# A state-space loop on one core: where a group's output is added to x, and the order of two kinds of loads

## The chip, the cores and the metric

The kernel runs on one core of a Trainium2 chip. The metric is the device time of one execution in microseconds. The run shown is one profiled execution; beside it stand three unprofiled ones. All times inside the execution count from the start of its span.

## The reference, cut to what matters

A stack of six layers on x of shape (4, 256, 512), all float32: a mixture-of-experts layer, an attention layer, the same experts again, a SwiGLU layer, a Mamba2 layer, the same SwiGLU again. The change is in the Mamba2 layer:

```python
proj = hidden_states @ in_proj_w.T                  # gate, x/B/C, dt
xBC = silu(conv(xBC) + conv_b)                      # depthwise, 4 taps
scores = einsum('bclhn,bcshn->bchls', C, B) * exp(seg)   # per head, lower triangle
y = scores @ (x * dt) + carried state + x * D
yg = y * silu(gate)
rstd = rsqrt(mean(yg**2 over the 1024 channels of a group) + 1e-5)
out = (yg * rstd * norm_w) @ out_proj_w.T
x = x + out
```

There are 128 heads of 64 channels, in 8 groups of 16 heads. The factor rstd belongs to one token and one group, so it can be applied after the output product: each group's 1024 channels give a (tokens x 512) sum, and this sum times rstd is added to x.

## The kernel before, in words

The 1024 tokens are 8 tiles of 128. The Mamba2 layer is a loop over 8 groups g (NG), each of 8 steps v (TPG); a step handles one pair of heads, 128 channels. All 64 steps are written out in program order on each engine, in a function `step(v, g)` that every engine has its own version of. Matrix products are float32 in three passes of high and low parts.

- **TensorE** (`step` in the block of `pe`): two input products (`chunk`) for the next step's channels; in even steps the second half (tiles 4 to 7) of the output products of the two steps before (`out_products`, half 1), and in step 0 also the sums of squares of the group before; then the attention-like products y of this step (`y_products`); two more chunks; transposes; in odd steps the first half (tiles 0 to 3) of the output products. An output product of a tile goes to one of three PSUM banks (OBANK), so product t + 3 waits until tile t has been read out. Products of the steps (0, 1), (2, 3), (4, 5), (6, 7) are summed in SBUF in `oacc`.
- **VectorE** (`step` in the block of `dve`), in this order: convolution taps (`taps`, L1393) of the first two chunks, in even steps with the read-out (`evacuate`) of tiles 4 to 7 between them; `skip` (L1446) and `gate` (L1455) on y; the low parts `y_lo` (L1461), each behind a high part that ScalarE writes (L913); `decay_off` (L1432), `scale_x` (L1411, L1413) for the next step; in odd steps the read-out of tiles 0 to 3; `decay` (L1439) for the next step, which that step's y products wait for. Step 7 has eight chunks of the next group in place of four.
- **The read-out** of the pair (0, 1) of a group is a copy into `oacc` (L1481), and the other pairs add to it (L1484). As the copy overwrites the sum of the group before, `update(g - 1, t)` (L1469), x + oacc * rstd for one tile, stands directly ahead of each of the eight copies: for tiles 0 to 3 at the end of step 1, for tiles 4 to 7 in step 2. The factor rstd comes in step 0 from TensorE (sums of squares), VectorE (L1489) and GpSimd (L607).
- **ScalarE**: weight high parts (L691), convolution starts (L862), the exponents of the decays (`spans`, L899, then Exp, L906), silu, y high parts.
- **GpSimd**: weight low parts (L551, L557), squares of y (L597, L601, L603), rstd (L607).
- **SyncE** issues all loads in one order (`step` in the block of `sp`): in step v the input weight slabs that TensorE uses from step v + 1 on (`mamba_A`, L363, 256 KB each; two in most steps, four in step 6), then the decay rows of the next step (`mamba_rows`, L404, 1.5 MB, broadcast to all partitions), then in even steps two output weight slabs (`mamba_B`, L373). A slab waits until the products that use its slot's last content are done; the rows wait for the y products of the step before this one.

Of the kernel before, what the change touches and what calls it, by code (L numbers as in the profile page):

```python
# [47 lines left out]
def build(nc, x_in, w0_in, b0_in, lb_in, wqkv_in, wo_in, fa_in, fb_in, ma_in, mb_in, dtw_in, chp_in, cst_in, out):  # L48
# [268 lines left out]
    def next_step(v, g):  # L317
        return (v + 1, g) if v < TPG - 1 else (0, g + 1)

    def step_chunks(v, g, last):  # L320
        if v < TPG - 1:
            return g, [4 + 4 * (v + 1) + c for c in range(4)]
        return g + 1, [] if last else list(range(8))

    def step_tiles(v, last):

        if v < TPG - 2:
            return [2 + 2 * (v + 2), 3 + 2 * (v + 2)]
        if last:
            return []  # L330
        return [NA_G + i for i in (range(4) if v == TPG - 2 else (4, 5))]
# [6 lines left out]
    def _(sp):  # L338
# [50 lines left out]
        def mamba_A(i, g):  # L389

            src = ma_in[g * NA_G + i] if isinstance(g, int) else ma_in[bass.ds(g * NA_G + i, 1)].squeeze(0)
            load_A(A0G + i, src, g, NA_G)

        def mamba_B(i, g):
            src = mb_in[g * TPG + i] if isinstance(g, int) else mb_in[bass.ds(g * TPG + i, 1)].squeeze(0)
            load_B(B0G + i, src, g, TPG)

        def mamba_rows(v, g):

            k = g * TPG + v  # L400
            if not (isinstance(k, int) and k < 2):
                sp.wait_ge(m_y, 2 * (k - 1) + FREE)
            h = slice(2 * k, 2 * k + 2) if isinstance(k, int) else bass.ds(2 * k, 2)
            sp.dma_start(eb[:, v % 2, :, :, :], scr[h].partition_broadcast(P)).then_inc(m_rows[v % 2], 16)  # L404

        def step(v, g, last=False):

            for i in step_tiles(v, last):
                mamba_A(i, g)
            mamba_rows(*next_step(v, g))  # L410
            if v % 2 == 0 and not (last and v == TPG - 2):
                mamba_B(v + 2, g)
                mamba_B(v + 3, g)
# [32 lines left out]
        for g in range(NG - 1):  # L446
            for v in range(1, TPG):
                step(v, g)
            step(0, g + 1)
# [660 lines left out]
    def _(dve):  # L1110
# [260 lines left out]
        def param(g, tile, which):  # L1371
            if tile < 2:
                at = CP_BC + tile * PBC + which
                per = 2 * PBC
            else:
                at = (tile - 2) // 2 * PX + which
                per = TPG * PX
            if isinstance(g, int):
                at = at + g * per
                return chp[:, at:at + 1]  # L1380
            return chp[:, bass.ds(g * per + at, 1)]

        def taps(g, c, which=(1, 2, 3)):

            n = conv_index(g, c)
            acc = conv_acc(g, c).rearrange("p (b l) -> p b l", b=2)
            src = ps[:, chunk_bank(g, c), :].rearrange("p (b l) -> p b l", b=2)
            for j in which:
                if j == 1:
                    dve.wait_ge(m_acc, n + 1)  # L1390
                else:
                    dve.wait_ge(m_tap, 3 * n + j - 1)
                nc.vector.scalar_tensor_tensor(out=acc[:, :, j:S], in0=src[:, :, 0:S - j],  # L1393
                                               scalar=param(g, c // 2, 3 - j), in1=acc[:, :, j:S],
                                               op0=ALU.mult, op1=ALU.add).then_inc(m_tap, 1)
# [21 lines left out]
        def decay_off(v, g, p):  # L1417

            k = g * TPG + v
            if k == 0:  # L1420
                dve.wait_ge(m_first[p], 48)
                dve.wait_ge(m_exp, p + 1)
            elif k == 1:
                dve.wait_ge(m_second, 32)
                dve.wait_ge(m_exp, 3)
            else:
                dve.wait_ge(m_rows[v % 2], 16 * (k // 2 + v % 2))
            if v == 0:
                dve.wait_ge(m_cbm, B * (g + 1))
            e = eb[:, v % 2, :, NT + 2 * p:NT + 2 * p + 2, :].rearrange("p h t q -> p h (t q)")  # L1430
            w = cbO[:, 2 * p:2 * p + 2, :].rearrange("p t q -> p (t q)")
            nc.vector.tensor_tensor(e, e, w.unsqueeze(1).to_broadcast([P, 2, 2 * P]), ALU.mult)  # L1432
# [25 lines left out]
        def y_lo(g, v, p):  # L1458
            half = slice(512 * p, 512 * p + 512)
            dve.wait_ge(m_yhi, 2 * (g * TPG + v) + p + 1 + FREE)  # L1460
            nc.vector.scalar_tensor_tensor(out=yTl[:, v % 2, half], in0=gt[:, v % 2, half],  # L1461
                                           scalar=param(g, 2 + 2 * v, 6), in1=yTh[:, v % 2, half].bitcast(F32),
                                           op0=ALU.mult, op1=ALU.subtract).then_inc(m_ylo, 1)

        def update(g, t):
            if t % 4 == 0:
                dve.wait_ge(m_rstd, g + 1 + FREE)
            dve.wait_ge(m_osum, 32 * g + 24 + t + 1 + FREE)
            nc.vector.scalar_tensor_tensor(out=x[:, t, :], in0=oacc[:, t, :], scalar=rstd[:, t:t + 1],  # L1469
                                           in1=x[:, t, :], op0=ALU.mult, op1=ALU.add).then_inc(x_new, 1)  # L1470

        def evacuate(v, g, t):

            j = v // 2
            done = 8 * j + t + 1
            dve.wait_ge(m_out, g * (NT * TPG // 2) + OB + done)
            if j == 0:
                if not (isinstance(g, int) and g == 0):
                    update(g - 1, t)
                    dve.wait_ge(x_new, g * NT + XB[4] + t + 1)  # L1480
                nc.vector.tensor_copy(oacc[:, t, :], ps[:, OBANK[t % 3], :]).then_inc(m_osum, 1)  # L1481
            else:
                dve.wait_ge(m_osum, 32 * g + done - 8 + FREE)
                nc.vector.tensor_tensor(oacc[:, t, :], ps[:, OBANK[t % 3], :], oacc[:, t, :],  # L1484
                                        ALU.add).then_inc(m_osum, 1)

        def mean_square(g, bank):
            dve.wait_ge(m_ss, g + 1 + FREE)
            nc.vector.tensor_scalar(ss[:, :], ps[:, bank, 0:NT], 1.0 / GROUP, EPS, ALU.mult,  # L1489
                                    ALU.add).then_inc(m_var, 1)  # L1490
# [47 lines left out]
        def step(v, g, last=False, first=False):  # L1538
            gn, todo = step_chunks(v, g, last)
            conv = [c for c in todo if c < 4 or (c // 2) % 2 == 0]  # L1540
            drain = v % 2 == 0 and not first
            before = (v - 1, g) if v else (TPG - 1, g - 1)
            taps(gn, conv[0])
            taps(gn, conv[1], (1,))
            if drain:
                evacuate(*before, 4)
            taps(gn, conv[1], (2, 3))
            if drain:
                for t in range(5, NT):
                    evacuate(*before, t)  # L1550
                if v == 0:
                    mean_square(g - 1, 4)
            ending = last and v == TPG - 2
            if ending:
                decay_off(v + 1, g, 0)
                decay_off(v + 1, g, 1)
            skip(g, v, 0)
            gate(g, v, 0)
            skip(g, v, 1)
            gate(g, v, 1)  # L1560
            if ending:
                decay(v + 1, g, 0)
                decay(v + 1, g, 1)
                scale_x(v + 1, g, 0)
                scale_x(v + 1, g, 1)
            if len(conv) > 2:
                taps(gn, conv[2])
            y_lo(g, v, 0)
            if len(conv) > 2:
                taps(gn, conv[3])  # L1570
            y_lo(g, v, 1)
            if len(conv) > 2:
                taps(gn, conv[4])
                taps(gn, conv[5])
                for b in range(B):
                    mask_cb(gn, b)
            vn = next_step(v, g)
            if not ending and not (first and v == 0):
                decay_off(*vn, 0)
                decay_off(*vn, 1)  # L1580
            if not ending:
                scale_x(*vn, 0)
                scale_x(*vn, 1)
            if v % 2 == 1:
                for t in range(4):
                    evacuate(v, g, t)
            if first and v == 0:
                decay_off(*vn, 0)
                decay_off(*vn, 1)
            if not ending:  # L1590
                decay(*vn, 0)
                decay(*vn, 1)
# [693 lines left out]
```

## Time and profile before

| | |
|---|---|
| median of 3 runs | 2223.58 us (2219.56 to 2225.03) |
| the profiled execution, its own time | 2223.88 us |
| its span | 2222.1 us |
| mean granted TensorE clock | 0.989 |
| busy: TensorE, weight loads | 96%, 79% |
| busy: VectorE, ScalarE, GpSimd | 75%, 65%, 46% |

The span is what the profiler sees; the execution's own time is 1.8 us longer. The loop over groups and steps takes most of the span from 570 to 2010 us, 184 to 186 us a group. A busy share is an average over stages with different limits, so the reading goes stage by stage. A line of the windows view gives a stretch, its length, the busy time (and instructions) of TensorE, its weight loads, VectorE, ScalarE and GpSimd, then the granted TensorE clock, the DMA engines' share and GB/s. A line of the timeline gives start, duration, engine, source line, operation, tiles and, in brackets, the idle time before it with what ended it. "ps" are the PSUM banks, "wBh,yTh" an output product, "xTh,wAh" an input product, "eb,xdt" a y product.

### The profile page before, as it was taken

To read this page: it belongs to the slowest core of one execution; us is meant where nothing else is said; L and a number is where in the kernel's file an instruction comes from. 1 tells how busy PE (TensorE), PEld (TensorE's weight loads), DVE (VectorE), ACT (ScalarE), POOL (GpSimd) and SP (SyncE) were. 2 spreads that over 40 slices of the span, in tenths; PEclk is the share of its full clock that TensorE was granted. 3 is DMA by queue.
4 is the path that set the end of the run, shared out by engine and by line. 5 is a ranking of instruction groups with operands and counts; after the bars stand their busy time and mean duration, and the time that the engine had idled before them with its cause. 6 is when DMAs were issued, how large, how long until landed. Compare 5 with 4: busy or idle time off the path is not lost.

```text
span 2222.1 us, 34801 instructions
## 1 busy us (share of the span) xinstructions
PE 2141.8 (96%) x12604; PEld 1750.1 (79%) x12604; DVE 1660.0 (75%) x2661; ACT 1434.2 (65%) x3090; POOL 1031.9 (46%) x755
## 2 busy tenths in 40 slices
PE   7989889999999999999999999999999999998999
PEld 7866678887788878878878887887887888787887
DVE  7777673225888898899889889889888988987121
ACT  4488643335978767668776776767867677683332
POOL 5577445352354345344454434534445443454442
PEclk9999999999999999999999999999999999999999
DMA  3000012331432323233224232323322432231332
GB/s 133 1 1 2 1 44 86 95 93 54 153 131 102 110 95 109 94 120 117 93 86 142 94 117 86 109 99 115 124 86 86 143 106 104 86 110 48 95 95 81
DMA packets 65337, 202.53 MB, mean 91 GB/s; under 512 B 7056, under 2 KB 9104, under 8 KB 56976
## 3 DMA queue, kind: packets, MB, share of 16 engines
q1 hardware_dynamic: 65168, 200.31, 26.6%
q8 instruction: 102, 1.67, 0.3%
q14 instruction: 67, 0.55, 0.1%
HBM read 197.39 MB, written 2.88 MB: 90 GB/s over the span
## 4 chain that ended last, share of the span: by engine, by line
PE 74%; DVE 12%; ACT 8%; issue 4%; DMA 1%; POOL 0%; SPq 0%; DVEq 0%; ACTq 0%; POOLq 0%
PE ps L1678 70%; ACT eb L899 2%; DVE x L1469 2%; DVE eb L1439 2%; PE ps L1982 2%; PE ps L1800 2%; DVE work L1393 1%; DMA eb<-scr_decays 1%; PE ps L1693 1%; DVE PT L1305 1%; ACT eb L906 1%; DVE eb L1432 1%; DVE yTl L1461 1%; DVE xdt L1411 1%; DVE nm L1283 1%
## 5 line engine op out<-in xcount | busy, mean ns | idle before, releaser
L551 POOL TENSOR_TENSOR wAl<-rawA,wAh 128x512 fp32r<-128x512 f32 x233 | 324.3, 1404 | 399.2 <-ACT wAh L691 398.7
L1678 PE MATMUL ps<-xTh,wAh 128*128 128x512 f32 x1512 | 426.4, 403 | 8.9 <-DVE work L1393 3.2
L1678 PE MATMUL ps<-xTl,wAh 128*128 128x512 f32 x1512 | 415.2, 396 | 0.0
L1678 PE MATMUL ps<-xTh,wAl 128*128 128x512 f32 x1512 | 415.2, 396 | 0.0
L1393 DVE SCALAR_TENSOR_TENSOR work<-ps,chp,work 128x510 f32<-128x510 f32 (+2 forms) x465 | 343.5, 744 | 45.7 <-ACT work L862 35.7
L1678 PEld LDWEIGHTS ps<-xTh,wAl 128*128 128x128 f32 x1512 | 284.7, 188 | 69.6
L1678 PEld LDWEIGHTS ps<-xTh,wAh 128*128 128x128 f32 x1512 | 275.9, 189 | 80.2 <-issue 20.1
L1678 PEld LDWEIGHTS ps<-xTl,wAh 128*128 128x128 f32 x1512 | 284.4, 188 | 69.4
L557 POOL TENSOR_TENSOR wBl<-rawB,wBh 128x512 fp32r<-128x512 f32 x108 | 141.6, 1324 | 386.0 <-ACT wBh L695 386.0
L899 ACT ACTIVATE eb<-eb,gc 128x128 f32<-128x128 f32 x1008 | 307.7, 392 | 12.9 <-DMA eb<-scr_decays 12.9
L601 POOL TENSOR_TENSOR sqt<-gt 128x512 f32<-128x512 f32 x110 | 152.4, 1385 | 116.7 <-DVE gt L1455 108.2
L862 ACT ACTIVATE work<-ps,gpar 128x512 f32<-128x512 f32 x155 | 119.3, 770 | 128.7 <-PE ps L1678 94.0
L1439 DVE TENSOR_TENSOR eb<-eb,cbD 128x1024 f32<-128x1024 f32 x128 | 195.3, 1565 | 4.3 <-ACT eb L906 4.3
L1347 DVE TENSOR_TENSOR hs<-ps,gs 128x512 f32<-128x512 f32 x44 | 30.4, 692 | 224.5 <-PE ps L1678 188.2
L603 POOL TENSOR_TENSOR sq<-sq,sqt 128x512 f32<-128x512 f32 x110 | 187.4, 1704 | 8.6
L1678 PE MATMUL ps<-wBh,yTh 128*128 128x512 f32 x512 | 166.1, 404 | 16.7 <-DVE oacc L1481 16.6
L1678 PE MATMUL ps<-eb,xdt 128*64 128x128 f32 x2048 | 163.0, 281 | 7.6 <-DVE eb L1439 6.1
L1678 PE MATMUL ps<-wBh,yTl 128*128 128x512 f32 x512 | 161.2, 395 | 0.0
L1678 PE MATMUL ps<-wBl,yTh 128*128 128x512 f32 x512 | 161.1, 394 | 0.0
L691 ACT ACTIVATE wAh<-rawA 128x512 fp32r<-128x512 f32 x233 | 142.4, 620 | 24.6 <-DMA rawA<-fa_in 23.1
L1461 DVE SCALAR_TENSOR_TENSOR yTl<-gt,chp,yTh 128x512 fp32r<-128x512 f32 x128 | 124.8, 978 | 44.1 <-ACT yTh L913 43.1
L913 ACT ACTIVATE yTh<-gt,gpar 128x512 fp32r<-128x512 f32 x128 | 91.0, 716 | 99.7 <-DVE gt L1455 99.0
(208 smaller groups left out, 3979.0 us busy)
## 6 DMA issues: line engine op xcount, KB each, us to landing
eb<-scr_decays SPq DMA_DIRECT2D x62, 1536.0 KB, 6.4
rawA<-ma_in SPq DMA_DIRECT2D x144, 256.0 KB, 3.6
rawA<-fa_in SPq DMA_DIRECT2D x88, 256.0 KB, 2.6
rawB<-mb_in SPq DMA_DIRECT2D x64, 256.0 KB, 2.9
rawB<-fb_in SPq DMA_DIRECT2D x44, 256.0 KB, 2.6
x<-x_in SPq DMA_DIRECT2D x8, 256.0 KB, 6.4
x_out<-x SPq DMA_DIRECT2D x8, 256.0 KB, 2.7
wqraw<-wqkv_in SPq DMA_DIRECT2D x1, 1536.0 KB, 11.4
```

The source lines that it names most:

```text
L551: nc.gpsimd.tensor_tensor(wAl[:, slot, :], rawA[:, slot, :], wAh[:, slot, :].bitcast(F32), ALU.subtract).then_inc(A_lo, 1)
L557: nc.gpsimd.tensor_tensor(wBl[:, slot, :], rawB[:, slot, :], wBh[:, slot, :].bitcast(F32), ALU.subtract).then_inc(B_lo, 1)
L601: nc.gpsimd.tensor_tensor(sqt[:, :], y, y, ALU.mult).then_inc(m_sqt, 1)
L603: nc.gpsimd.tensor_tensor(sq[:, half], sq[:, half], sqt[:, :], ALU.add).then_inc(m_sq, 1)
L691: nc.scalar.activation(wAh[:, n % SLOTA, :], rawA[:, n % SLOTA, :], ACT.Copy).then_inc(A_hi, 1)
L862: nc.scalar.activation(conv_acc(g, c), ps[:, chunk_bank(g, c), :], ACT.Identity, bias=param(slot, c // 2, 4), scale=param(slot, c // 2, 3) ...
L899: last = nc.scalar.activation(eb[:, v % 2, h, t, :], eb[:, v % 2, h, t, :], ACT.Relu, bias=start, scale=-1.0)
L913: nc.scalar.activation(yTh[:, v % 2, half], gt[:, v % 2, half], ACT.Copy, scale=param(0, 2 + 2 * v, 6)).then_inc(m_yhi, 1)
L1393: nc.vector.scalar_tensor_tensor(out=acc[:, :, j:S], in0=src[:, :, 0:S - j], scalar=param(g, c // 2, 3 - j), in1=acc[:, :, j:S], op0=ALU.m ...
L1439: nc.vector.tensor_tensor(e, e, w.unsqueeze(1).to_broadcast([P, 2, 4 * P]), ALU.mult).then_inc(m_s, 1)
L1461: nc.vector.scalar_tensor_tensor(out=yTl[:, v % 2, half], in0=gt[:, v % 2, half], scalar=param(g, 2 + 2 * v, 6), in1=yTh[:, v % 2, half].b ...
L1678: return nc.tensor.matmul(o, l, r, start=start, stop=end, **kw)
```

## The change

Three places. SyncE issues the rows of the next step ahead of the slabs. `evacuate` of the first pair no longer calls `update`. In VectorE's step 0, `update` is called for tiles 0 and 1 after the first `y_lo` and for tiles 2, 3 and 4 after the second; in step 1 for tiles 5, 6 and 7 after the second.

```diff
@@ sync: step(v, g, last) @@
+            mamba_rows(*next_step(v, g))
             for i in step_tiles(v, last):
                 mamba_A(i, g)
-            mamba_rows(*next_step(v, g))
             if v % 2 == 0 and not (last and v == TPG - 2):
                 mamba_B(v + 2, g)
                 mamba_B(v + 3, g)
@@ vector: evacuate(v, g, t) @@
             if j == 0:
-                if not (isinstance(g, int) and g == 0):
-                    update(g - 1, t)
+                if g > 0:
                     dve.wait_ge(x_new, g * NT + XB[4] + t + 1)
                 nc.vector.tensor_copy(oacc[:, t, :], ps[:, OBANK[t % 3], :]).then_inc(m_osum, 1)
@@ vector: step(v, g, last, first) @@
             y_lo(g, v, 0)
+            if v == 0 and g > 0:
+                for t in range(2):
+                    update(g - 1, t)
             if len(conv) > 2:
                 taps(gn, conv[3])
             y_lo(g, v, 1)
+            if v < 2 and g > 0:
+                for t in range(2 + 3 * v, 5 + 3 * v):
+                    update(g - 1, t)
             if len(conv) > 2:
                 taps(gn, conv[4])
                 taps(gn, conv[5])
```

## Rows read from the trace of the kernel before

**Rows 1.** Windows, y(1) to y(3), then y(3) to y(5) of group 2.
```profile
770.75:816.33 45.58, 43.19 (x258) 34.80 (x257) 43.20 (x55) 31.56 (x63) 21.35 (x15) 0.96 0.30 105
...
1323.79:1369.36 45.57, 43.21 (x257) 34.82 (x256) 43.19 (x55) 31.56 (x63) 21.37 (x15) 0.96 0.30 104
1509.64:1554.20 44.56, 41.68 (x257) 33.56 (x256) 42.18 (x55) 32.12 (x65) 20.86 (x15) 1.00 0.30 107
...
1000.66:1041.85 41.19, 41.19 (x257) 33.66 (x256) 37.56 (x51) 31.55 (x63) 20.25 (x14) 1.00 0.34 116
```
**Rows 2.** Waits in the loop: us in total, times, longest us.
```profile
PE ps L1678 <- DVE oacc L1481: 16.6, 14, 2.0
...
ACT eb L899 <- DMA eb<-scr_decays: 12.9, 7, 2.8
```
**Rows 3.** Timeline of TensorE, group 2: products of tile 3, tile 7; tile 3 in step 3.
```profile
969.16 0.74 PE L1678 MATMUL ps<-wBh,yTh 128*128 128x512 f32 x2 [0.43 <-DVE oacc L1481]
...
982.46 0.73 PE L1678 MATMUL ps<-wBh,yTh 128*128 128x512 f32 x2 [1.92 <-DVE oacc L1481]
...
1014.17 0.74 PE L1678 MATMUL ps<-wBh,yTh 128*128 128x512 f32 x2
```
**Rows 4.** Timeline of VectorE, group 2, steps 0 to 2.
```profile
947.16 0.75 DVE L1461 SCALAR_TENSOR_TENSOR yTl<-gt,chp,yTh 128x512 fp32r<-128x512 f32 x1 [1.73 <-ACT yTh L913]
...
951.73 2.36 DVE L1439 TENSOR_TENSOR eb<-eb,cbD 128x1024 f32<-128x1024 f32 x2 [0.61 <-ACT eb L906]
...
956.87 2.31 DVE L1393 SCALAR_TENSOR_TENSOR work<-ps,chp,work 128x510 f32<-128x510 f32 x3 [0.56 <-ACT work L862]
...
962.81 0.75 DVE L1461 SCALAR_TENSOR_TENSOR yTl<-gt,chp,yTh 128x512 fp32r<-128x512 f32 x1 [0.87 <-ACT yTh L913]
963.90 0.75 DVE L1461 SCALAR_TENSOR_TENSOR yTl<-gt,chp,yTh 128x512 fp32r<-128x512 f32 x1 [0.34 <-ACT yTh L913]
...
967.63 0.74 DVE L1469 SCALAR_TENSOR_TENSOR x<-oacc,rstd,x 128x512 f32<-128x512 f32 x1
968.41 0.69 DVE L1481 COPY oacc<-ps 128x512 f32<-128x512 f32 x1
969.02 1.09 DVE L1469 SCALAR_TENSOR_TENSOR x<-oacc,rstd,x 128x512 f32<-128x512 f32 x1
...
973.91 3.57 DVE L1439 TENSOR_TENSOR eb<-eb,cbD 128x1024 f32<-128x1024 f32 x2
...
981.72 0.69 DVE L1481 COPY oacc<-ps 128x512 f32<-128x512 f32 x1
```
**Rows 5.** Timeline of GpSimd, group 2, step 0 and end of step 1.
```profile
940.40 1.66 POOL L607 TENSOR_TENSOR rstd<-ss,cst 128x8 f32<-128x8 f32 x1 [4.45 <-DVE ss L1489]
...
953.24 2.00 POOL L551 TENSOR_TENSOR wAl<-rawA,wAh 128x512 fp32r<-128x512 f32 x1 [6.91 <-ACT wAh L691]
...
968.28 2.99 POOL L557 TENSOR_TENSOR wBl<-rawB,wBh 128x512 fp32r<-128x512 f32 x2 [9.56 <-ACT wBh L695]
```
**Rows 6.** Windows, start of y(7) to y(0) of the next group.
```profile
1267.20:1308.74 41.54, 41.54 (x233) 34.65 (x232) 35.15 (x54) 30.62 (x64) 13.10 (x10) 1.00 0.15 54
1451.56:1494.59 43.03, 41.80 (x234) 34.62 (x233) 35.15 (x54) 30.63 (x64) 13.08 (x10) 1.00 0.16 52
...
1821.10:1864.01 42.91, 41.81 (x233) 34.63 (x232) 35.15 (x54) 30.62 (x64) 13.09 (x10) 1.00 0.15 52
```
**Rows 7.** Timeline of ScalarE: slab high part in step 1, exponents in step 7.
```profile
952.55 0.61 ACT L691 ACTIVATE wAh<-rawA 128x512 fp32r<-128x512 f32 x1
...
1638.21 2.45 ACT L899 ACTIVATE eb<-eb,gc 128x128 f32<-128x128 f32 x8 [2.48 <-DMA eb<-scr_decays]
```
**Rows 8.** Timeline of SyncE's queue: decay rows in step 1 and in step 7.
```profile
942.93 0.33 SPq L404 DMA_DIRECT2D eb<-scr_decays  x1
...
1630.50 0.43 SPq L404 DMA_DIRECT2D eb<-scr_decays  x1
```

## The prediction, made before the changed kernel was run

> **What bounds the kernel now.** I read the loop, not the page's shares: TensorE is the engine that sets its time, so the question is where it waits, and the waits in the loop answer that. Of the waits that touch this change, its matmuls wait for VectorE's copies into oacc 14 times, 16.6 us in all, twice in each of the seven groups that have a group before them [rows 2]. The timeline shows the places: the output product of tile 3 in step 1, after 0.43 us of idle time, and that of tile 7 in step 2, after 1.92 us [rows 3]. Each needs the PSUM bank that a copy empties, and the copy stands behind an `update` on VectorE [rows 4]. The windows view tells what this costs. From y(1) to y(3) a group takes 45.58 us in groups 1 to 4 (first and last row of the four) and 44.56 in groups 5 to 7 (one row of three alike), against 41.19 from y(3) to y(5), the same work with no update in it [rows 1]. The difference between the two kinds is the clock: 0.96 granted against 1.00. In 45.6 us that is 3.6 us at the lower of the two levels (1.2 GHz in place of 2.4), and it follows the idle time before tile 7; after the same idle time it didn't fall in the other three groups. It costs 1.0 us (45.58 less 44.56).
>
> A second loss is in step 7. From y(7) to the next y(0) groups 1 to 3 take 41.54 us, but groups 4 to 6 43.03 to 42.91, two of the three shown [rows 6]. There ScalarE waits 2.48 us for the decay rows, issued at 1630.50 [rows 7, 8]; over the loop it waits seven times, 12.9 us [rows 2].
>
> **Part 1, SyncE's order.** The rows of a step may go once the y products of the step before are done, but in steps 6, 7 and 0 they stand behind slabs that wait for two more chunks, some 6 us after y. Put first, they go those 6 us earlier. ScalarE's wait of at most 2.8 us goes away, and with it some 1.4 us in each of the three long groups (43.03 and 42.91 less 41.54): **-4.2 us**. In groups 1 to 3 and at other steps the wait hid behind TensorE, so nothing is gained. What is moved back: the slabs. In steps 1, 3 and 5 they now follow 1.5 MB. The rows are issued at 942.93, and ScalarE takes the first slab at 952.55, 9.62 us later [rows 7, 8]; rows at 1630.50 land by 1638.21, in 7.7 us [rows 7, 8]. One slab of a sixth of the size behind them adds about 1.3 us by that row: 9.0 us, just in time. So I cost it at nothing, from below nothing (rows earlier) to what the slower rival says. The output slabs on the same queue wait for products far later and lose nothing.
>
> **Part 2, VectorE, group 2 as the example.**
> - Step 0. The first y_lo ends at 945.43 (947.16 less the idle 1.73), and rstd is ready at 942.06, so the new wait for it is free [rows 4, 5]. Two updates of 0.74 fit into the 1.73; a square on GpSimd may lengthen one as at 969.02, to 1.09 [rows 4], and 1.09 + 0.74 is 0.1 too long. Three more follow at about 0.67 from start to start (0.74 less the overlap that a copy of 0.69 shows, 968.41 to 969.02): 2.0. The idle 0.61 before the decays takes some back. 0.1 + 2.0 - 0.6: they start 1.5 us late, at 953.2.
> - The decays. Then they lie beside GpSimd's low part, which starts at 953.24 [rows 5]. Two decays take 2.36 us nearly alone and 3.57 beside GpSimd's work in step 2 [rows 4]. The bounds are 0 and 1.2; I take 1.2, since the low part is there at the very start of them. VectorE leaves step 0 late by 2.7 us. The y products of step 1 find the first decay done, the second up to 0.5 us late; that is inside the next item.
> - Step 1. VectorE has idle times of 0.56, 0.87 and 0.34 up to its second y_lo [rows 4], 1.77 in all, so 0.9 remains. Then three updates (2.0) come before the copy of tile 0, and one (0.78, 967.63 to 968.41) no longer does. That copy is late by 0.9 + 2.0 - 0.8 = **2.1 us**, and the product of tile 3 with it, whose idle time grows from 0.43 to about 2.3 less what y(1) has moved.
> - Step 2. The copy of tile 4 loses an update that took over 1.3 us, and three before it. It would be done by about 981, while tile 7's turn comes at 980.4 + 2.1. That wait goes.
> - From tile 3 to y(3) it takes 31.5 us now (969.16 to 1000.66) and 27.7 in the undisturbed steps (1014.17 to 1041.85) [rows 1, 3]. So the gain is 3.8 - 2.1 = 1.7 us in groups 1 to 4. In groups 5 to 7, where there was no 1.0 of slow clock to lose, it is 0.7. Together 4 x 1.7 + 3 x 0.7 = **-8.9 us**.
> - The clock. An idle time of 1.92 was followed by a fall in four groups of seven; one of about 2.1 now stands before tile 3. There input products follow, which run at the full rate, so a fall costs more than the 1.0 seen and at most half of 3.6 us; I take 1.4. Bounds: no group, seven groups. I take three: **+4.2 us**.
>
> Here a rule bears. The 3.57 against 2.36 shows that the engines get into each other's way. The Trainium skill (SBUF — State Buffer, "SBUF: two separate sides") says VectorE and GpSimd share a port pair that one instruction holds to its end, with VectorE counted where both inputs are in SBUF. By it a decay waits out the rest of one low part, of up to 1.5 us (2.99 for two [rows 5]), and the sum is as above or 0.3 us a group worse; without it the decays are not late and the first rival holds.
>
> **Sum**: -4.2 - 8.9 + 4.2 = -8.9 on the profiled execution's own 2223.88 us, so 2215; the median is 0.3 us below it, and I say **2214**. About 0.3%, 6.7 us, is what a measurement of this kernel can tell from no change; that limit is at 2216.9.
>
> **The rivals.**
> - *No collision in step 0* (0.25). If the updates find gaps between GpSimd's instructions and the decays stay at 2.36, VectorE's lateness of 1.5 is gone within 1.77 of idle time. The copy is then late by 2.0 - 0.8 = 1.2 us, the gain is 2.6 and 1.6 us a group, 15.2 in all, and an idle time of 1.6 lowers the clock in no group: 2223.6 - 4.2 - 15.2 = 2204. For it: in step 0 most of GpSimd's time is idle, 6.91 us before 953.24 [rows 5]. Against: the low part's place.
> - *The stall only moves* (0.12). The clock falls in six or seven groups after tile 3, 9 us in place of 4.2, or VectorE is half a microsecond later still: 2218 to 2221. For it: the idle time is longer than the one that lowered it four times.
> - *The rows' order gains nothing* (0.08): the long steps 7 have another cause, as 41.8 us of 43.03 is busy time, a little over the 41.54 elsewhere [rows 6]. Then 2218.
> - *Slower: the slabs come late* (0.07). Place: ScalarE's first slab in steps 1, 3, 5. If it lands later than 9.6 us after the rows' issue, ScalarE's whole step is late, 24 times. If nothing hides it, the loss passes the gain of 9 us at 0.4 us each, so at 10.0 us; at 10.8 the kernel takes 2223.6 - 9 + 24 x 1.2 = 2243. For it: only 0.6 us between my 9.0 and 9.6. Against: ScalarE and VectorE have idle time in those steps.
>
> My forecast has 0.48: some two thirds of it below 2216.9 (up to four falls of the clock), the rest above. **Chances**: faster 0.25 + 0.37 = 0.62; same 0.11 + 0.12 + 0.08 = 0.31; slower 0.07. **Range**: my own case spans 2209 (no fall) to 2218; down to the first rival and up to the stall that moves it is 2203 to 2221.
>
> **What would show it.** Right: no idle time before tile 7 in step 2; one of about 2 us before tile 3 in step 1; 43 to 44 us from y(1) to y(3) where the clock stays full; 41.5 us from y(7) to y(0) in all groups; no wait of ScalarE for rows; decays of step 0 near 3.5 us. Wrong: an idle time before tile 3 well under 2 us (first rival), ScalarE waiting for input slabs (slower rival), y(1) later than 15.6 us after y(0), or GpSimd's rstd arriving after VectorE asks for it.

## The result, and the profile after

| | before | after |
|---|---|---|
| median | 2223.34 us (4 runs, 2219.56 to 2225.03) | 2201.09 us (4 runs, 2200.18 to 2201.96) |
| the profiled execution, its own time | 2223.88 us | 2201.61 us |
| its span | 2222.1 us | 2199.8 us |
| mean granted TensorE clock | 0.989 | 0.995 |
| busy: VectorE, GpSimd | 75%, 46% | 75%, 47% |

The ratio is 0.9904, with an interval of 0.989 to 0.9919. The changed kernel is faster by 22 us. The forecast was 2214 with a range from 2203 to 2221, so the time lies 13 us below the forecast and 2 us below the range. It is the first rival that came, with its 2204.

The first view is the windows of the changed kernel, with the columns of before: y(1) to y(3) of groups 1 and 5, then y(3) to y(5) of group 2, then y(7) to y(0) after groups 3 and 6.

```profile
769.25:812.18 42.93, 41.30 (x257) 33.66 (x256) 39.37 (x54) 31.44 (x63) 21.63 (x15) 1.00 0.32 111
...
1495.40:1538.33 42.93, 41.30 (x258) 33.65 (x257) 39.38 (x54) 31.44 (x63) 21.62 (x15) 1.00 0.33 111
...
993.72:1034.76 41.04, 41.04 (x257) 33.73 (x256) 35.97 (x49) 31.44 (x63) 20.73 (x15) 1.00 0.34 116
...
1257.31:1298.80 41.49, 41.49 (x233) 34.79 (x233) 35.24 (x54) 29.63 (x62) 13.10 (x10) 1.00 0.16 53
...
1801.95:1843.45 41.50, 41.50 (x234) 34.80 (x233) 35.24 (x54) 29.65 (x62) 13.09 (x10) 1.00 0.16 53
```

Two things are to be seen against [rows 1] and [rows 6]. Step 7 takes the same 41.5 us everywhere; the three long ones of 42.7 to 43.0 are gone. And y(1) to y(3) takes 42.93 to 42.97 in all seven groups, at the full clock in every one. Before, it was 45.58 in groups 1 to 4 and 44.56 in groups 5 to 7.

A table of the stretches shows where the 22.3 us between the two profiled executions (2223.88 less 2201.61) came from. Each entry is a difference between starts of y products:

| stretch | before | after | gain |
|---|---|---|---|
| y(1) to y(4), groups 1 to 4 | 71.72 | 68.94 | 4 x 2.8 = 11.1 |
| y(1) to y(4), groups 5 to 7 | 70.78 | 68.92 | 3 x 1.9 = 5.6 |
| y(7) to y(0), after groups 4, 5, 6 | 43.03, 42.68, 42.91 | 41.49 each | 4.2 |
| span's start to y(0) of group 0 | 569.86 | 568.41 | 1.5 |

The last line isn't the change's doing. The updates begin in group 1, and what stands ahead of y(0) of group 0 does the same work in all kernels of this study. Up to 326 us the changed kernel is 0.9 us behind; from 348 us on it is 1.5 us ahead. Between the two, the clock fell in the execution before and not in the one after. The windows view of before, then of after, shows it:

```profile
320.00:350.00 30.00, 26.20 (x130) 21.81 (x129) 17.33 (x57) 13.96 (x26) 13.27 (x14) 0.89 0.14 45
```

```profile
320.00:350.00 30.00, 26.21 (x143) 22.17 (x142) 19.17 (x63) 15.03 (x27) 14.65 (x16) 1.00 0.15 45
```

Over all profiled executions, y(0) of group 0 starts at 569.6 to 571.0 us where this stretch has 0.89 (four of them) and at 568.4 to 569.3 where it has 1.00 (seven). So a difference of 1.5 us between two kernels can be this stretch alone.

The waits of the changed kernel hold one line of the two in [rows 2] (us in total, times, longest); ScalarE's wait for the decay rows, 12.9 us before, is on the list no more:

```profile
PE ps L1683 <- DVE oacc L1480: 11.4, 7, 1.6
```

Seven waits are left, one in each group, and the timeline of TensorE in group 2 shows that it is tile 3's in step 1. Tile 7, which waited 1.92 us [rows 3], waits no longer.

```profile
966.04 0.74 PE L1683 MATMUL ps<-wBh,yTh 128*128 128x512 f32 x2 [1.63 <-DVE oacc L1480]
```

The timeline of VectorE in the same group shows the moved updates (L1469), the decays of steps 0 and 1 (L1439), the copies of tiles 0 to 2 into oacc (L1480) and the one of tile 4:

```profile
941.04 2.19 DVE L1469 SCALAR_TENSOR_TENSOR x<-oacc,rstd,x 128x512 f32<-128x512 f32 x2
943.15 0.74 DVE L1461 SCALAR_TENSOR_TENSOR yTl<-gt,chp,yTh 128x512 fp32r<-128x512 f32 x1
943.81 2.06 DVE L1469 SCALAR_TENSOR_TENSOR x<-oacc,rstd,x 128x512 f32<-128x512 f32 x3
...
948.87 2.34 DVE L1439 TENSOR_TENSOR eb<-eb,cbD 128x1024 f32<-128x1024 f32 x2
951.13 4.51 DVE L1393 SCALAR_TENSOR_TENSOR work<-ps,chp,work 128x510 f32<-128x510 f32 x6
...
959.58 0.75 DVE L1461 SCALAR_TENSOR_TENSOR yTl<-gt,chp,yTh 128x512 fp32r<-128x512 f32 x1 [0.34 <-ACT yTh L913]
960.25 2.07 DVE L1469 SCALAR_TENSOR_TENSOR x<-oacc,rstd,x 128x512 f32<-128x512 f32 x3
...
965.31 1.87 DVE L1480 COPY oacc<-ps 128x512 f32<-128x512 f32 x3
...
968.34 3.56 DVE L1439 TENSOR_TENSOR eb<-eb,cbD 128x1024 f32<-128x1024 f32 x2
...
975.02 0.68 DVE L1480 COPY oacc<-ps 128x512 f32<-128x512 f32 x1
```

And GpSimd beside them:

```profile
948.92 3.43 POOL L551 TENSOR_TENSOR wAl<-rawA,wAh 128x512 fp32r<-128x512 f32 x1 [6.91 <-ACT wAh L691]
953.12 1.29 POOL L551 TENSOR_TENSOR wAl<-rawA,wAh 128x512 fp32r<-128x512 f32 x1 [0.77 <-ACT wAh L691]
```

This is the pair of lines that decided the forecast. Group 2's y(0) stood at 940.05 before and stands at 935.73 now, so times are compared from y(0) on. The decays of step 0 start 13.14 us after it, against 11.68 before: 1.46 late. The low part of GpSimd starts 0.05 us after them, and so it does in all seven groups (0.05 to 0.06). Its span is 3.43 us where the next one, alone, takes 1.29. The decays take 2.34 us, as undisturbed as in [rows 4]. The engines did meet, but it was GpSimd that paid, and nobody waits for it there.

### The profile page after: what moved, and what is told of

It is laid out like the page before. It is cut to its first block, busy times and chain, and to the rows that moved or that the text cites. A ratio compares the mean times of both kernels' runs of the same rounds, so it can differ in the third digit from the quotient of the medians.

```text
span 2199.8 us, 34805 instructions
## 1 busy us (share of the span) xinstructions
PE 2129.0 (97%) x12594; PEld 1744.9 (79%) x12604; DVE 1642.6 (75%) x2661; ACT 1431.4 (65%) x3090; POOL 1038.7 (47%) x755
## 4 chain that ended last, share of the span: by engine, by line
PE 83%; ACT 7%; DVE 6%; issue 3%; DMA 0%; POOL 0%; DVEq 0%; ACTq 0%; SPq 0%; POOLq 0%
PE ps L1683 78%; ACT eb L899 2%; PE ps L1987 2%; PE ps L1805 2%; PE ps L1698 1%; DVE PT L1305 1%; ACT eb L906 1%; DVE nm L1283 1%; ACT yTh L913 1%; ACT work L862 0%; DVE eb L1432 0%; ACT wAh L691 0%; ACT xc L878 0%; ACT pr_a L772 0%; DVE bst L1125 0%
## 5 line engine op out<-in xcount | busy, mean ns | idle before, releaser
L551 POOL TENSOR_TENSOR wAl<-rawA,wAh 128x512 fp32r<-128x512 f32 x233 | 339.6, 1470 | 382.5 <-ACT wAh L691 381.7
L601 POOL TENSOR_TENSOR sqt<-gt 128x512 f32<-128x512 f32 x110 | 149.5, 1360 | 97.6 <-DVE gt L1455 89.2
L1439 DVE TENSOR_TENSOR eb<-eb,cbD 128x1024 f32<-128x1024 f32 x128 | 190.2, 1524 | 0.0
L603 POOL TENSOR_TENSOR sq<-sq,sqt 128x512 f32<-128x512 f32 x110 | 185.1, 1683 | 8.6
L886 ACT ACTIVATE gt<-ps 128x512 f32<-128x512 f32 x128 | 75.8, 592 | 124.3 <-PE ps L1683 76.9
L1461 DVE SCALAR_TENSOR_TENSOR yTl<-gt,chp,yTh 128x512 fp32r<-128x512 f32 x128 | 120.0, 938 | 42.7 <-ACT yTh L913 42.0
## 6 DMA issues: line engine op xcount, KB each, us to landing
wqraw<-wqkv_in SPq DMA_DIRECT2D x1, 1536.0 KB, 10.8
```

Source lines behind the costliest of these rows:

```text
L551: nc.gpsimd.tensor_tensor(wAl[:, slot, :], rawA[:, slot, :], wAh[:, slot, :].bitcast(F32), ALU.subtract).then_inc(A_lo, 1)
L601: nc.gpsimd.tensor_tensor(sqt[:, :], y, y, ALU.mult).then_inc(m_sqt, 1)
L603: nc.gpsimd.tensor_tensor(sq[:, half], sq[:, half], sqt[:, :], ALU.add).then_inc(m_sq, 1)
L886: nc.scalar.activation(gt[:, v % 2, 512 * (c % 2):512 * (c % 2) + 512], ps[:, chunk_bank(g, c), :], ACT.Silu).then_inc(m_gate, 1)
```

## The experiments

Eight variants were run, and the changed kernel a second time. Diffs are against the changed kernel unless said otherwise. The steps given are differences between starts of y products, in us. The changed kernel's are: y(0) to y(1) 15.05, y(1) to y(2) 27.90, y(2) to y(3) 15.03, y(3) to y(4) 26.0.

### Each part alone

**The new order of SyncE alone**: the kernel before, with only this edit.

```diff
+            mamba_rows(*next_step(v, g))
             for i in step_tiles(v, last):
                 mamba_A(i, g)
-            mamba_rows(*next_step(v, g))
```

> The kernel before with SyncE's order alone changed. Theory (the two parts add up): only the long step 7 of groups 4 to 6 goes, so y(7) to y(0) is 41.5 us in all groups, y(1) to y(3) stays at 44.6 to 45.6, and the time is 2223.3 - 4.2 = 2219. Rival (the long step 7 has another cause): 2223, with ScalarE's wait for the decay rows gone and y(7) to y(0) still near 43 in three groups.

Measured: 2220.47 us (2220.11 to 2224.85, 11 runs), ratio 0.9999 (0.999 to 1.0008) to a kernel before of 2221.94: no difference that can be measured. The wait went all the same. The windows of this kernel: y(7) to y(0) after group 4, then y(1) to y(3) of groups 1, 5 and 7.

```profile
1451.32:1492.81 41.49, 41.49 (x234) 34.79 (x233) 35.24 (x54) 29.63 (x62) 13.09 (x10) 1.00 0.16 56
...
770.54:816.10 45.56, 43.21 (x257) 34.79 (x256) 43.17 (x55) 31.55 (x63) 21.37 (x15) 0.96 0.30 105
...
1507.86:1553.41 45.55, 43.18 (x257) 34.73 (x256) 43.16 (x55) 31.55 (x63) 21.37 (x15) 0.96 0.29 105
...
1876.54:1922.10 45.56, 43.18 (x257) 34.73 (x257) 43.18 (x55) 31.55 (x63) 21.14 (x15) 0.96 0.31 105
```

Step 7 takes 41.49 in every group, ScalarE's wait for the rows is gone, and 4.2 us with it. But in groups 5 to 7, where y(1) to y(3) took 44.56 at the full clock, it now takes 45.55 at 0.96. The same idle time before tile 7 was followed by a fall of the clock in four groups of seven before, and in seven of seven here. Three times 1.0 us was given back, which leaves 1.2. The other executions go the same way: the mean granted clock is 0.988 over the 11 of this kernel and 0.991 over 21 of the kernel before.

**The updates alone**: the changed kernel with SyncE's old order.

> The changed kernel with SyncE's old order. Theory: all of the rest, 16.7 us by the step intervals, comes from the moved updates: 2201.1 + 4.2 = 2205.3, y(1) to y(3) 42.9 us in all seven groups. Rival (the parts need each other: the earlier decay rows also helped VectorE in steps 0 and 1): y(1) to y(3) over 43.5 and the time over 2208.

Measured: 2206.03 us (2202.34 to 2207.41, 5 runs), ratio 0.9924 (0.9911 to 0.9938). From y(1) to y(3) every group takes 42.93, as in the changed kernel. Step 7 is long again, in groups 1, 4, 5 and 6 (42.22, 42.45, 42.61 and 42.98 against 41.49: 4.3 us), and ScalarE waits for the rows 12.9 us as before. Its window after group 5:

```profile
1622.59:1665.20 42.61, 41.80 (x233) 34.62 (x232) 35.16 (x54) 30.63 (x64) 13.09 (x10) 1.00 0.16 54
```

So in the changed kernel SyncE's order is worth 4.9 us by the medians (2206.03 less 2201.09) and 4.3 by the stretches of these two kernels. On the kernel before it is worth nothing that can be measured. The parts don't add up, because the clock takes back what the first gives as long as the idle time before tile 7 is there.

### What is left to gain

**No updates.** The groups' outputs are never added to x, for groups 0 to 6; the rest is done.

```diff
@@ evacuate @@
-                    dve.wait_ge(x_new, g * NT + XB[4] + t + 1)
+                    dve.sem_inc(x_new, 1)
@@ step @@
-            if v == 0 and g > 0:
-                for t in range(2):
-                    update(g - 1, t)
...
-            if v < 2 and g > 0:
-                for t in range(2 + 3 * v, 5 + 3 * v):
-                    update(g - 1, t)
```

> The changed kernel without the updates of groups 0 to 6, so their output is never added to x: what the updates still cost. Theory (the idle time before tile 3 is made by the three updates of step 1 and nothing else): it goes, y(1) to y(2) falls from 27.90 to 26.1, and the time is 2201.1 - 7 x 1.8 = 2188.5. Rival (another wait of about the same place stands behind it, ScalarE's high parts): at most half of that, 2195.

Measured: 2189.33 us (2188.92 to 2189.82, 4 runs), ratio 0.9853 (0.9838 to 0.9868). From y(1) to y(2) it takes 26.00 in place of 27.90. All other steps are those of the changed kernel to 0.05 us. So the updates in their new places still cost 1.9 us a group, about 12 us by the medians, and all of it stands between y(1) and y(2), where tile 3 waits 1.63 us. I take this kernel as the floor for any order of them.

**Updates 5 to 7 behind the copies of step 1**, ahead of the decays.

```diff
-            if v < 2 and g > 0:
-                for t in range(2 + 3 * v, 5 + 3 * v):
+            if v == 0 and g > 0:
+                for t in range(2, 5):
                     update(g - 1, t)
...
             if v % 2 == 1:
                 for t in range(4):
                     evacuate(v, g, t)
+            if v == 1 and g > 0:
+                for t in range(5, NT):
+                    update(g - 1, t)
```

> The changed kernel with the three updates of tiles 5 to 7 behind the copies of tiles 0 to 3 in step 1, ahead of the decays, in place of ahead of them. Theory: VectorE's decays of step 1 are made some 7 us before they are needed, so the updates are free there: the copy of tile 0 comes 2.0 us earlier, the idle time before tile 3 goes, the copy of tile 4 comes at the same time as now while tile 7's turn is 1.8 us earlier, which costs up to 0.2 us; y(1) to y(2) 26.1 to 26.3, time 2189 to 2190. Rival (VectorE has no room between tile 3 and tile 7, the wait only moves on to tile 7): y(1) to y(2) stays over 27.5, time 2199 to 2201.

Measured: 2224.14 us (2220.95 to 2229.33, 11 runs), ratio 1.0013 (1.0004 to 1.0022). Both expectations missed by over 20 us. The timeline of VectorE in group 3:

```profile
1156.76 3.90 DVE L1469 SCALAR_TENSOR_TENSOR x<-oacc,rstd,x 128x512 f32<-128x512 f32 x3
1160.58 4.29 DVE L1439 TENSOR_TENSOR eb<-eb,cbD 128x1024 f32<-128x1024 f32 x2
```

GpSimd beside it squares y of step 1 and adds (L601, L603), then makes low parts:

```profile
1156.82 1.59 POOL L601 TENSOR_TENSOR sqt<-gt 128x512 f32<-128x512 f32 x1
...
1161.64 2.15 POOL L603 TENSOR_TENSOR sq<-sq,sqt 128x512 f32<-128x512 f32 x1
1163.75 3.50 POOL L551 TENSOR_TENSOR wAl<-rawA,wAh 128x512 fp32r<-128x512 f32 x2
```

And TensorE at tile 7 of the same group:

```profile
1168.40 0.73 PE L1686 MATMUL ps<-wBh,yTh 128*128 128x512 f32 x2 [2.58 <-DVE oacc L1480]
```

Three updates that take 2.07 us in the changed kernel take 3.90 here, and the two decays 4.29. From y(1) to y(2) it took 28.9 to 31.3 us, and the clock fell in five groups of seven (1, 2, 3, 5 and 6).

The seven groups, with the same code, went two ways. In groups 3, 4, 5 and 7 the first update starts 30.68 us after y(0), and it is the square beside it that is lengthened (0.74 and 1.59 us). In groups 1, 2 and 6 it starts at 30.70 to 30.72, and the update is (1.6 and 1.04 us), though by the trace it still starts before the square, which stands at 30.72 to 30.74 in all seven. The three updates and the square in group 2:

```profile
970.52 4.76 DVE L1469 SCALAR_TENSOR_TENSOR x<-oacc,rstd,x 128x512 f32<-128x512 f32 x3
```

```profile
970.54 1.04 POOL L601 TENSOR_TENSOR sqt<-gt 128x512 f32<-128x512 f32 x1
```

Some hundredths of a microsecond separate the three groups in which tile 7 waits 3.7 us from the four in which it waits 2.58.

The place was empty of waits and full of another engine's work; I had counted VectorE's instructions at their undisturbed 0.7 us and left out what runs beside them.

**Updates 5 to 7 directly ahead of their own copies** in step 2, where the kernel before had them, with 0 to 4 as in the changed kernel.

```diff
             if j == 0:
                 if g > 0:
+                    if t >= 5:
+                        update(g - 1, t)
...
-            if v < 2 and g > 0:
-                for t in range(2 + 3 * v, 5 + 3 * v):
+            if v == 0 and g > 0:
+                for t in range(2, 5):
                     update(g - 1, t)
```

> The changed kernel with the updates of tiles 5, 6 and 7 directly ahead of their own copies in step 2 again; those of tiles 0 to 4 stay in step 0. Theory (an update costs little where GpSimd rests, and much beside it: in the run with the updates behind the copies three of them took 3.90 us and the decays 4.29, in place of 2.07 and 3.56): in step 2 GpSimd is done by then, so the updates take 0.75 each. The idle time before tile 3 goes (1.8 us a group), y(1) to y(2) is 26.0 to 26.2, y(2) to y(3) 15.0 to 15.6, and the time is 2189 to 2193. Rival (any update between the product of tile 3 and y(3) costs its length): 2.1 us a group come back, 2203.

Measured: 2194.63 us (2192.37 to 2195.99, 4 runs), ratio 0.9876 (0.986 to 0.9893). The wait of tile 3 is gone, and y(1) to y(2) takes 26.01. Something came back behind it: y(2) to y(3) takes 15.63 where it takes 15.03, as y(3) waits for VectorE's decays, and y(3) to y(4) takes 26.2 where it takes 26.0. The timelines of VectorE and TensorE show one update beside a low part (the others at this place take 0.74), and the wait:

```profile
974.98 1.28 DVE L1469 SCALAR_TENSOR_TENSOR x<-oacc,rstd,x 128x512 f32<-128x512 f32 x1
```

```profile
992.24 0.66 PE L1685 MATMUL ps<-eb,xdt 128*64 128x128 f32 x8 [0.53 <-DVE eb L1439]
```

**One update in the gap of step 1, two ahead of their copies.** The gap between the two y_lo of step 1 is idle for 0.34 us in the changed kernel and can hold update 5 in part; 6 and 7 stay with their copies.

```diff
                 if g > 0:
+                    if t >= 6:
+                        update(g - 1, t)
...
             if v == 0 and g > 0:
                 for t in range(2):
                     update(g - 1, t)
+            if v == 1 and g > 0:
+                update(g - 1, 5)
...
-            if v < 2 and g > 0:
-                for t in range(2 + 3 * v, 5 + 3 * v):
+            if v == 0 and g > 0:
+                for t in range(2, 5):
                     update(g - 1, t)
```

> The version with updates 5, 6 and 7 ahead of their own copies in step 2 (2194.6 us), but update 5 in step 1 between the two low parts, where VectorE had 0.35 us of idle time; 0 to 4 in step 0, 6 and 7 ahead of their copies. Theory: update 5 costs 0.67 less 0.35 there, some 0.1 us before tile 3; in step 2 VectorE is 0.75 and more earlier, also past the weight split that lengthened update 5 to 1.28, so y(2) to y(3) falls from 15.63 to 15.03 and y(3) to y(4) from 26.2 to 26.0: 2194.6 - 7 x 0.7 = 2190. Rival (the last 5 us over the run without updates aren't the lateness of VectorE in step 2): 2194 to 2196.

Measured: 2190.56 us (2189.47 to 2192.49, 4 runs), ratio 0.9854 (0.9838 to 0.9871). The changed kernel, run again on the same chip, took 2201.59 (2201.28 to 2201.79, 4 runs):

> The changed kernel once more, on this chip, as a yardstick for the version beside it. Theory: 2201 and no fall of the clock in the loop, as in the first result. Rival (that the clock stayed full was luck of one execution): a clock fall in some groups, 1.5 us each, and a spread of over 3 us between runs.

So this version is 11 us faster than the change and has the ratio of the kernel that leaves the updates out (0.9853), though y(1) to y(2) still takes 0.15 us more than there in each of seven groups. The timeline of VectorE, step 1 and step 2 of group 2:

```profile
959.35 0.75 DVE L1469 SCALAR_TENSOR_TENSOR x<-oacc,rstd,x 128x512 f32<-128x512 f32 x1
...
963.74 1.88 DVE L1482 COPY oacc<-ps 128x512 f32<-128x512 f32 x3
...
976.45 0.74 DVE L1469 SCALAR_TENSOR_TENSOR x<-oacc,rstd,x 128x512 f32<-128x512 f32 x1
977.23 0.69 DVE L1482 COPY oacc<-ps 128x512 f32<-128x512 f32 x1
977.84 0.74 DVE L1469 SCALAR_TENSOR_TENSOR x<-oacc,rstd,x 128x512 f32<-128x512 f32 x1
978.61 0.69 DVE L1482 COPY oacc<-ps 128x512 f32<-128x512 f32 x1
```

All updates are at 0.75 or less but the first in step 0, which takes 1.53 as it does in the changed kernel (1.52). The copy of tile 0 starts 27.82 us after y(0) (963.74 less 935.92) in place of 29.58, and TensorE has no idle time before tile 3 or tile 7. The steps are 26.15, 15.03 and 26.0.

### The forecast's own case, made to happen

The prediction had the decays of step 0 start just behind the low part. The changed kernel has them just ahead of it. **One update in the first gap in place of two, four behind the second y_lo in place of three** should shift them by what tells the two apart.

```diff
             if v == 0 and g > 0:
-                for t in range(2):
+                for t in range(1):
                     update(g - 1, t)
...
             if v < 2 and g > 0:
-                for t in range(2 + 3 * v, 5 + 3 * v):
+                for t in range(1 + 4 * v, 5 + 3 * v):
                     update(g - 1, t)
```

> The changed kernel with one update in the first gap of step 0 and four behind the second low part, in place of two and three, so that the decays of step 0 start some 0.3 us later. Theory (whichever of VectorE and GpSimd is first holds the other up): the low part on GpSimd, which started 0.05 us after the decays, now starts first; the pair of decays takes about 3.2 us in place of 2.34, the low part 1.3 in place of 3.43, y(1) comes up to 0.6 us late, and the idle time before tile 3 grows by up to 1 us: 2204 to 2210, and more where the clock falls. Rival (VectorE always goes first here): decays 2.34, low part over 3 us, at most 0.3 us a group: 2201 to 2203.

Measured: 2215.1 us (2213.97 to 2216.08, 8 runs), ratio 0.9968 (0.9957 to 0.9979); it is 13.5 us slower than the changed kernel in its second run (2201.59), with the same instructions. VectorE's decays of step 0 in group 2:

```profile
950.60 3.19 DVE L1439 TENSOR_TENSOR eb<-eb,cbD 128x1024 f32<-128x1024 f32 x2
```

GpSimd's low part, now 0.31 us ahead of them:

```profile
950.29 1.29 POOL L551 TENSOR_TENSOR wAl<-rawA,wAh 128x512 fp32r<-128x512 f32 x1 [6.91 <-ACT wAh L691]
```

The roles have changed: the low part takes 1.29, the decays 3.19. TensorE shows what follows, a wait of y(1) for the first decay and then the wait of tile 3:

```profile
952.72 0.66 PE L1683 MATMUL ps<-eb,xdt 128*64 128x128 f32 x8 [0.50 <-DVE eb L1439]
...
968.24 1.11 PE L1683 MATMUL ps<-wBh,yTh 128*128 128x512 f32 x2 [1.92 <-DVE oacc L1480]
```

The windows of y(1) to y(3), groups 1 and 2:

```profile
770.35:813.56 43.21, 41.28 (x256) 33.69 (x257) 39.94 (x54) 31.09 (x61) 20.06 (x14) 1.00 0.32 110
...
952.72:997.48 44.76, 42.84 (x256) 34.80 (x257) 40.17 (x54) 31.08 (x61) 20.19 (x14) 0.96 0.30 106
```

The 13.5 us have three terms: y(1) comes 0.57 later after y(0) in each group (4.0); y(1) to y(2) takes 28.17 at the full clock against 27.90 (7 x 0.27 = 1.9); and in five groups of seven the clock falls after tile 3, at 1.55 each (7.8). Their sum is 13.7.

**The squares of step 1 made small**, in the kernel before. GpSimd squares and adds 8 columns in place of 512 in step 1, so most of that step's part of the sum of squares is left out.

```diff
-                nc.gpsimd.tensor_tensor(sqt[:, :], y, y, ALU.mult).then_inc(m_sqt, 1)
+                n = 8 if v == 1 else 512
+                part = slice(512 * p, 512 * p + n)
+                nc.gpsimd.tensor_tensor(sqt[:, 0:n], gt[:, v % 2, part], gt[:, v % 2, part], ALU.mult).then_inc(m_sqt, 1)
                 pool.wait_ge(m_sqt, k)
-                nc.gpsimd.tensor_tensor(sq[:, half], sq[:, half], sqt[:, :], ALU.add).then_inc(m_sq, 1)
+                nc.gpsimd.tensor_tensor(sq[:, part], sq[:, part], sqt[:, 0:n], ALU.add).then_inc(m_sq, 1)
```

> The kernel before with GpSimd's four squares of every step 1 cut from 512 columns to 8, so these squares are left out of the sum: a measure of what the updates lost at their old place beside GpSimd. Theory: the two decays of step 1 fall from 3.57 us to about 2.4, the update before the copy of tile 4 from 1.41 to 0.75, so the idle time before tile 7 falls from 1.92 to 0.3 or less, the clock stays full, and the time is 2222 - 7 x 1.8 - 3 = 2206 to 2210. Rival (the updates' own length is what counted, not GpSimd): the time stays over 2218.

Measured: 2209.14 us (2207.35 to 2210.23, 4 runs), ratio 0.9944 (0.9927 to 0.996). VectorE's instructions are those of before. In group 2's read-out two of them changed their length by over 0.1 us, the decays ahead of y(2) and the update ahead of the copy of tile 4:

```profile
972.55 2.89 DVE L1441 TENSOR_TENSOR eb<-eb,cbD 128x1024 f32<-128x1024 f32 x2
...
978.24 0.74 DVE L1471 SCALAR_TENSOR_TENSOR x<-oacc,rstd,x 128x512 f32<-128x512 f32 x1
```

The decays took 3.57 in [rows 4], the update 1.41 at the same place. The decays are still 0.5 us over their undisturbed 2.36; a low part of GpSimd runs beside them. The timeline of TensorE at tiles 3 and 7:

```profile
967.88 0.73 PE L1680 MATMUL ps<-wBh,yTh 128*128 128x512 f32 x2 [0.43 <-DVE oacc L1483]
...
979.76 0.73 PE L1680 MATMUL ps<-wBh,yTh 128*128 128x512 f32 x2 [0.53 <-DVE oacc L1483]
```

Tile 7 waits 0.53 us in place of 1.92, and the clock falls in no group of seven. The expectation had 0.3 or less. Some 1.4 us of the old stall was therefore time that VectorE lost beside GpSimd, not work of its own. Without a single update moved, that alone, with the falls of the clock that followed it, gives 12.8 us (2221.98 less 2209.14).

## Why the prediction was wrong where it was, and right where it was

**The step that failed** is "The decays. ... I take 1.2, since the low part is there at the very start of them." The updates were to make the decays 1.5 us late, and 1.46 was measured (its parts were 0.3 from the first gap, where two updates took 2.19, and 0.8 taken back by idle times, for 0.1 and 0.6). From rows of one execution I set them at 953.2 and the low part at 953.24, which is a tie, and then priced only the case in which VectorE loses it. The trace shows the other: 948.87 against 948.92, the low part taking 3.43 us and the decays 2.34. The loser of this tie is VectorE, with the whole path to tile 3 behind it, or GpSimd, whose next low part has idle time ahead of it in any case (2.19 us before, 0.77 after). [rows 5] held a sign: the low part took 2.00 us there, against 1.29 for the next one, as the second decay had started 0.4 us ahead of it. GpSimd was the one that waited in the kernel before, too. Moving one update over by one place gave the other case (3.19 and 1.29) and 2215.1 us, where the forecast for it was 2214. The mechanism was right, and the wrong side of it was taken. With both starts 0.04 us apart by my own working, the chances of the two should have been near equal; 0.48 against 0.25 wasn't. (The split of the 0.48 has a slip besides: 0.37 of it is some three quarters, not two thirds.)

Here the rule that the forecast weighed can be judged. With starts 0.05 us apart one way and 0.31 the other, the one that starts first was undisturbed in both runs, and the other was longer by most of what was left: 3.43 against 1.29, and 3.19 against 2.34. The Trainium skill (SBUF — State Buffer, "SBUF: two separate sides") says that the first gets the shared pair for its whole instruction and the other blocks. By that rule, these two traces agree on who waits. They don't agree on how long, as the low part waited for two instructions and not one, and the run with the updates behind the copies shows that starts some hundredths apart in a trace don't tell who was first. In the prediction I read it as speaking only against the change; it speaks against whichever engine is second.

**What followed from it.** The lateness of 2.7 us behind the decays was 1.5. The idle time of step 1 took all of it back, so 0 was carried on and not 0.9. The copy of tile 0 was late by 1.2 us against y(0) (29.58 after it, from 28.36) and not by 2.1. Tile 3's idle time was 1.63, not 1.9 or more, and the clock fell in no group. The terms then are those of the first rival, though not for its reason, as the decays did meet the low part: 2.6 and 1.6 us a group; 2.8 and 1.9 were measured. Its terms hold from y(1) to y(3) (45.58 less 42.93 is 2.65, and 44.56 less 42.93 is 1.63). Some 0.2 more a group lies between y(3) and y(4), 26.15 to 26.2 before and 25.98 to 26.02 now; no forecast of the changed kernel had it. It goes with the updates ahead of their copies in step 2: with three or four of them there it takes 26.2 (own copies; the kernel before and the small squares), with two or none 26.0. How it comes about wasn't tried. That is 1.3 us in all, and with the 1.5 us ahead of the loop it is what the rival's 2204 lacked. The 13.4 us between my 2215 and the profiled 2201.6 are thus 6.3 for the decays (7 x 0.9, the 1.2 less the 0.3 that made no difference), 4.2 for the clock, 1.3 and 1.5.

**The clock term**, +4.2 for three falls, was zero. In the case I had assumed it was larger than I took: five groups at 1.55, 7.8 us. My 2214 for that case was close because two errors met. Without the clock, groups 1 to 4 gained 1.95 us there and groups 5 to 7 1.0, 10.8 in all where I had 8.9; so the sum is -4.2 - 10.8 + 7.8 = -7.2, against my -8.9. The rest of the distance to 2215.1 lies before and behind the loop.

**SyncE's order**: -4.2 was forecast, and it is -4.2 by the stretches against the kernel before, -4.3 against the updates alone and -4.9 by the medians. Alone it gives 1.2 by the stretches, and that I had not seen: the prediction took it as a term that adds up. The rival that gave the long steps 7 another cause is refuted, as they take 41.49 us in every group once the rows go first.

**The slabs** were not late. The DMA issues of the changed kernel's page (KB each, median us from issue to landing) show both transfers:

```profile
eb<-scr_decays SPq DMA_DIRECT2D x62, 1536.0 KB, 6.5
rawA<-ma_in SPq DMA_DIRECT2D x144, 256.0 KB, 6.8
```

A slab took 3.6 us before and 6.8 behind the rows. The order alone does it: 6.8 with only SyncE's order changed, 3.7 with only the updates moved. In group 2, SyncE issues the rows at 938.62 and ScalarE takes the first slab at 948.23, 9.61 us later, and it waits for none there. My 9.0 for the landing was some 2 us too long, on the safe side. The slower rival is refuted.

**Tile 7** went as forecast: the copy of tile 4, which frees its bank, is at 975.02, before its turn, and no idle time is left there. **Stall only moves** was half right: the wait moved to tile 3, at 1.63, but took no clock with it.

## What to carry to other kernels

When two engines' instructions lengthen each other, and an edit shifts one of them by about as much as separates their starts, work out both orders and price both; a shift of the decays by 0.4 us (13.14 to 13.50 after y(0)) decided 13.5 us here. An idle place on one engine is only as good as what the other engine does in it: the updates cost 0.7 us each in step 1 of the changed kernel and 1.3 beside the squares. And a term won in one stage is safe only if no stall elsewhere sits on the edge of the clock's fall; remove that stall first.

## What was not expected of the hardware

- **The clock near its edge.** Idle times before an output product of 1.90 to 1.96 us were followed by a fall from 2.4 to 1.2 GHz for a stretch in 4 groups of 7 (before), 7 of 7 (SyncE's order alone) and 5 of 7 (one and four updates). 1.63 us was followed by one in none of 21 (the changed kernel twice, the updates alone), 2.58 in 2 of 4 and 3.7 in 3 of 3 (updates behind the copies). A fall after tile 7 cost 1.0 us, one after tile 3 cost 1.55. What decides between the groups with the same idle time stays open; no run varied it alone.
- **Two decays in a row pass a waiting low part.** In the changed kernel the low part waited until both decays were done (3.43 is 1.29 and 2.14, nearly the 2.34 of both), though it had asked 0.05 us into the first. At the end of step 1 the squares do get in between decays, and the two then take 3.56. And so does a low part in step 0 of group 0, in this kernel and all others. The timelines of VectorE and GpSimd there:

```profile
587.10 3.44 DVE L1439 TENSOR_TENSOR eb<-eb,cbD 128x1024 f32<-128x1024 f32 x2
```

```profile
587.33 2.13 POOL L551 TENSOR_TENSOR wAl<-rawA,wAh 128x512 fp32r<-128x512 f32 x1 [5.87 <-ACT wAh L691]
```

The same two instructions meet, but the low part starts 0.23 us into the first decay in place of 0.05, and it is done 1.1 us before the second decay ends. Whether the 0.23 is what gives it its turn, and why, wasn't tried, so it stays open.
- **The undisturbed loser.** A rival engine's wait can be free: GpSimd's 2.1 us in step 0 shows in no interval of TensorE: y(0) to y(1) takes 15.05 us before and after.
